# Query/key products directly behind their step's score pair, and their low parts ahead of the two maxima

## The reference

```python
h = _rmsnorm(x, norm_scale)
q = jnp.einsum('bsd,dhe->bshe', h, wq)       # 16 heads of 64
k = jnp.einsum('bsd,dhe->bshe', h, wk)
v = jnp.einsum('bsd,dhe->bshe', h, wv)
weights = jnp.einsum('bqhd,bkhd->bhqk', q * head_dim ** -0.5, k)
weights = jax.nn.softmax(weights, axis=-1)
new_vals = jnp.einsum('bhqk,bkhd->bqhd', weights, v)
out = jnp.einsum('bqhe,hed->bqd', new_vals, w_out) + b_out
...
x = _layernorm(x + _L0_attn_ref(x, ...))     # the first attention, above
x = _layernorm(x + _L0_ffn_ref(x, ...))      # 8 experts of 256, two chosen, and a shared one
x = _layernorm(x + _L1_attn_ref(x, ...))     # attention over the 16 heads of one token
x = _layernorm(x + _L1_ffn_ref(x, ...))      # 8 experts of 512, two chosen
```

## Time and profile before

| what | value |
|---|---|
| median of 3 runs | 1448.29 us (1448.22 to 1450.28) |
| the profiled execution, on the device | 1447.02 us |
| its span in the trace | 1445.2 us |
| TensorE matmuls busy | 1375.4 us, 95% of the span |
| TensorE weight loads busy | 1203.8 us, 83% |
| VectorE / ScalarE / GpSimd busy | 928.1 / 903.1 / 498.9 us |
| granted TensorE clock, mean | 0.988 |

### The profile page before, as it was taken

How to read it: one execution, slowest core, us unless ns; L and a number is a source line. 1 busy time by engine, 2 the same in 40 slices (tenths; PEclk the granted TensorE clock), 3 DMA queues, 4 the chain that set the end, 5 groups by cost and what they waited for, 6 DMA issues and landing times.

```text
span 1445.2 us, 33202 instructions
## 1 busy us (share of the span) xinstructions
PE 1375.4 (95%) x11328; PEld 1203.8 (83%) x11328; DVE 928.1 (64%) x2535; ACT 903.1 (62%) x2492; POOL 498.9 (35%) x409
## 2 busy tenths in 40 slices
PE   5797999999999999999999999999999999999768
PEld 4585989888898988889898898988889898888767
DVE  4456567575666757576675756667575675756683
ACT  4665775757566575766757576575757757575423
POOL 2307053160714417062350706225070531607100
PEclk9999999999999999999999999999999999999988
DMA  7000000000000000000000000000000000000000
GB/s 259 1 5 1 5 2 8 0 2 5 0 7 0 7 0 0 7 0 7 0 7 0 0 7 0 7 0 7 0 0 7 0 7 0 2 3 1 5 1 8
DMA packets 14088, 13.77 MB, mean 10 GB/s; under 512 B 1625, under 2 KB 12770, under 8 KB 13794
## 3 DMA queue, kind: packets, MB, share of 16 engines
q1 hardware_dynamic: 14050, 13.27, 2.9%
HBM read 11.17 MB, written 2.10 MB: 9 GB/s over the span
## 4 chain that ended last, share of the span: by engine, by line
PE 64%; issue 13%; DVE 8%; ACT 4%; DVEq 4%; POOL 3%; POOLq 2%; DMA 0%; SPq 0%; ACTq 0%
PE bank_F L1204 14%; PE bank_S L1074 6%; DVEq L343 4%; PE bank_T L1115 4%; PE bank_A L1128 4%; PE bank_T L1060 3%; ACT probs L566 3%; PE bank_A L1139 3%; PE bank_T L1061 3%; PE bank_T L1062 3%; PE bank_A L1060 3%; PE bank_A L1061 3%; PE bank_A L1062 3%; PE bank_F L1060 2%; PE bank_F L1062 2%
## 5 line engine op out<-in xcount | busy, mean ns | idle before, releaser
L1204 PE MATMUL bank_F<-down,hid 128*128 128x128 f32 x2944 | 356.0, 276 | 7.1 <-DVE x L783 6.4
L1204 PEld LDWEIGHTS bank_F<-down,hid 128*128 128x128 f32 x2944 | 341.5, 192 | 17.2 <-DVE x L783 9.9
L566 ACT ACTIVATE probs<-bank_S,neg_max 128x256 f32<-128x256 f32 x512 | 235.9, 475 | 143.6 <-DVE neg_max L704 143.6
L704 DVE TENSOR_REDUCE neg_max<-bank_S 128x2 f32<-128x512 f32 x256 | 164.7, 685 | 96.3 <-PE bank_S L1074 96.2
L783 DVE SCALAR_TENSOR_TENSOR x<-bank_F,gates,x 128x128 f32<-128x128 f32 x496 | 150.1, 344 | 42.5 <-PE bank_F L1204 32.7
L485 POOL TENSOR_TENSOR hid<-hid,qkv 128x1024 f32<-128x1024 f32 x60 | 169.1, 2828 | 22.7 <-ACT hid L582 22.7
L455 POOL TENSOR_TENSOR mean_sq<-sum_sq,one_over_d 128x2 f32<-128x2 f32 x16 | 3.1, 195 | 453.4 <-ACT h_row L540 453.4
L545 ACT ACTIVATE probsT<-bank_T 128x512 f32<-128x512 f32 x256 | 139.4, 605 | 28.0 <-PE bank_T L1115 28.0
L473 POOL TENSOR_TENSOR hid<-qkv 128x1024 f32<-128x1024 f32 x45 | 121.1, 2692 | 69.2 <-ACT qkv L545 69.2
L1139 PE MATMUL bank_A<-probsT,values 128*64 128x256 f32 x1024 | 140.4, 395 | 1.1 <-ACT probsT L545 1.0
L1115 PE MATMUL bank_T<-ident,probs 128*128 128x128 f32 x1024 | 138.3, 278 | 0.1
(11 more groups left out here) (191 smaller groups left out, 3233.2 us busy)
## 6 DMA issues: line engine op xcount, KB each, us to landing
x_row<-in_x SPq DMA_DIRECT2D x16, 128.0 KB, 2.1
down<-in_w SPq DMA_DIRECT2D x1, 2048.0 KB, 15.4
out<-x SPq DMA_DIRECT2D x16, 128.0 KB, 1.8
hid<-in_w SPq DMA_DIRECT2D x1, 1536.0 KB, 7.9
hid<-in_rw SPq DMA_DIRECT2D x1, 1024.0 KB, 7.4
hid<-in_wv SPq DMA_DIRECT2D x1, 512.0 KB, 3.9
hid<-in_wq SPq DMA_DIRECT2D x1, 512.0 KB, 4.8
hid<-in_wk SPq DMA_DIRECT2D x1, 512.0 KB, 5.5
```

What stands on the lines that cost most here:

```text
L566: ins = sc.activation(probs[:, h // 2 % 2, h % 2, t, :], unit.bank(f"S{h}")[:, t * S:(t + 1) * S], ACT.Exp, bias=neg_max[:, h, t:t + 1], a ...
L704: ve.tensor_reduce(neg_max[:, h, :], v.bank(f"S{h}")[:, :].rearrange("p (t k) -> p t k", t=NT), AX.X, ALU.max, negate=True).then_inc(max_r ...
L1204: ins = te.matmul(bank[:, (j * NT + t) * P:(j * NT + t + 1) * P], hid[:, e, k, tokens(t)], down[:, e, k, :], start=k == 0, stop=k == m - 1)
```

## The change

Two moves. In TensorE's list the unit `QK{s+3}` stands directly behind the score pair of step `s`, ahead of `O{s-1}` and the transposes, and no longer behind the transposes. In VectorE's step `lower_qk(s + 2)` stands ahead of the two maxima and no longer behind them. No instruction is added or taken away on any engine. ScalarE's list keeps its order.

```diff
@@ -87,11 +87,11 @@
         put("A", "QK2", on=a and s == 0)
         put("S0", f"S{2 * s + 2}", on=a and s + 1 < HP)
         put("S1", f"S{2 * s + 3}", on=a and s + 1 < HP)
+        put("A", f"QK{s + 3}", on=a and s + 3 < HP)
         put("A", f"O{s - 1}", on=a and s >= 1)
         put("F", *fill_units(it, s, 0))
         put("T0", f"T{2 * s}", on=a)
         put("T1", f"T{2 * s + 1}", on=a)
-        put("A", f"QK{s + 3}", on=a and s + 3 < HP)
         put("A", "HT", on=nxt and s == HP - 2)
         put("F", *fill_units(it, s, 1))
     put("A", f"O{HP - 1}", "OUT", on=a)
@@ -925,12 +925,11 @@
                 for s in range(HP):
                     if v.b and s == 3:
                         ln_apply(v, 1, x2, 1)
+                    if v.a and s + 2 < HP:
+                        lower_qk(v, s + 2)
                     if v.a and s + 1 < HP:
                         head_max(v, 2 * s + 2)
                         head_max(v, 2 * s + 3)
-
-                    if v.a and s + 2 < HP:
-                        lower_qk(v, s + 2)
                     if v.b and s == 0:
                         mix(v, "D0p1", 0, (2, 3), x2, x1, not v.a)
```

## The result

The changed kernel takes 1587.54 us (1584.82 to 1588.44), the kernel before, run beside it, 1448.78 us. The ratio is 1.0953 with a 95% interval of 1.0934 to 1.0972: 139 us slower. The prediction said slower, by 69 us, and 1538 us at most. The direction and nearly all waits were as predicted; the predicted loss was half of what came.

The account below looks back on a forecast made before the run. TensorE's own list was taken as the bound. Terms of 4.45 us a row over 15 rows, 66.8 us, plus 2.6 for row 0 made 69.4; added to 1447.0, plus 1.3 to the median, 1517.7 us, range 1498 to 1538.

Parts of the forecast that it names:

- row 0: First row, without fill units: `spread` of its step 5 gets the new wait, 2.6 us lost, bounds 0 and 4.45.
- 15 x 1.7: Waits in steps 3 and 4 over 15 rows: QK6 0.85, `spread` 0.2, QK7 0.8, less QK7's present wait 0.15 us.
- step 3 to 4: QK6 waits 0.85 us for the low part in step 3; `spread` of step 4 waits 0.2 us.
- step 4 to 5: QK7 waits 0.8 us, less its present wait of 0.15; `spread` of step 5 waits 0.95 us.
- `spread` of step 1: TensorE waits there for QK3's drain, ending with VectorE's low part of pair 3: stall of 2.2 us a row.
- the 0.2 us at `spread` of step 4: TensorE waits there for the scaling of O2, late because ScalarE's copy of x2's transpose is late: 0.2 us.
- Step 5, `spread`: TensorE waits for the low part of pair 7, queued behind VectorE's product of 1.27 us: 0.95 us a row.
- "No loss nor gain" behind step 5: Steps 6 and 7 have no QK unit; their VectorE chain moves with step 5's scores: neither loss nor gain.
- The credit of 0.4 us: Step 1: the mix comes 0.6 us earlier against the scores, so D0p3's wait goes: -0.4 us a row.
- The rival on the clock: The clock falls too: a 3 us half-clock stretch loses 1.5 us in each of 15 rows; 1540 us, chance 0.08.

Follow-up runs that it names:

- GpSimd late in after: Kernel after, with two small additions on GpSimd ahead of its second product so that VectorE's product starts first: 1552.41 us.
- banks kept: Kernel after, with every unit in the bank it had before and two small additions on GpSimd ahead of its second product: 1496.21 us.
- VectorE's half: Kernel before, with only the low part moved ahead of the maxima, plus two small additions on GpSimd ahead of its second product: 1469.71 us.
- GpSimd late in before: Kernel before, with only two small additions on GpSimd ahead of its second product: 1458.40 us.
- the tool: Two small additions on GpSimd ahead of its second product, result unused; alone on the kernel before: 1458.40 us.
- both undone: Kernel after, with two small additions on GpSimd ahead of its second product and unused matmuls (14 ahead of step 1, 6 ahead of step 5): 1533.90 us.
- VectorE's half alone: Kernel before, with only the low part moved ahead of the two maxima on VectorE, GpSimd unchanged: 1498.84 us.
- the version from the result: Kernel before, with VectorE's mixes of the older rows moved ahead of the maxima in steps 1, 2 and 5: 1441.88 us.
- TensorE's half alone: Kernel before, with only the QK units moved on TensorE, every unit in its old bank, VectorE's order untouched: 1630.21 us.

## Why the prediction was half right

The ladder of runs splits the 139 us, each rung being one edit (medians):

| from, to | us | what it is | predicted, 15 rows and row 0 |
|---|---|---|---|
| after to GpSimd late in after, 1587.5 to 1552.4 | 35 | product held off by GpSimd, and the clock lost with it | 0 |
| to banks kept, 1496.2 | 56 | re-dealt banks: `spread` of steps 1 and 5 | 15 x 3.15 + 2.6 = 50 |
| to VectorE's half, 1469.7 | 26.5 | TensorE's new order: QK units | 15 x 1.7 = 25.5 |
| to GpSimd late in before, 1458.4 | 11 | VectorE's new order | 15 x -0.4 = -6 |
| to before, 1448.8 | 10 | the tool | - |

The table says what each edit is worth in this order of undoing; the differences aren't strictly additive, since a stall can hide another edit's cost. Two of the rungs are known to be off. The tool's 10 us are those of the kernel before, where step 6 to 7 grows from 5.23 to 5.93 us; in the kernel after it stays at 5.17 us with the tool, so the first rung is 35 us, and some 3 more for the 0.2 us that the tool adds at the end of a row in either kernel. And VectorE's half carries that price while "banks kept" does not (6.00 and 5.29 us for the same step), so TensorE's new order costs, by estimate, 0.7 us a row more than its rung says, some 35 us.

A second account needs no ladder. It sets the steps of a row side by side, as means over rows 4 to 12 of the starts of `spread` in each trace (with both undone, over the seven of these rows that were undisturbed):

| stretch of a row | before | after | GpSimd late | both undone | predicted change |
|---|---|---|---|---|---|
| step 1 to 2 | 6.36 | 6.59 | 7.61 | 6.07 | -0.4 |
| step 2 to 3 | 7.77 | 7.96 | 7.96 | 7.96 | 0 |
| step 3 to 4 | 5.39 | 6.44 | 6.44 | 6.45 | 1.05 |
| step 4 to 5 | 5.85 | 9.76 | 7.65 | 7.65 | 1.6 |
| step 5 to 6 | 4.95 | 6.95 | 5.01 | 5.00 | 0 |
| step 6 to the last `spread` | 11.13 | 11.04 | 11.05 | 11.06 | 0 |
| from there to step 1 of the next row | 43.95 | 45.66 | 46.35 | 46.35 | 2.2 |
| row | 85.40 | 94.41 | 92.07 | 90.54 | 4.45 |

**The waits were right, and part of the closeness in the ladder is luck.** In row 6 it is 2.20 us for 2.2 at `spread` of step 1 and 1.06 for 1.05 from step 3 to 4. Each wait that came has the releaser that the prediction named; the 0.2 us at `spread` of step 4 did not come. TensorE was the bound, and of the stalls only 0.6 us a row were taken up later. The banks' rung is 56 us for 50, but not of the same things: it holds 1.5 us a row of lower clock behind step 1 (7.61 against 6.07 us), which the prediction left out, and it lacks 0.8 us for QK4, which waits only once the stall ahead of it is gone. Row 0 lost 3.7 us where 2.6 were predicted (the scores of step 0 of row 1 start at 93.20 and not at 89.51); the "0.47 us it waits now" in that working are the scaling and its hand-over, the wait itself is 0.53 us.

**Step 5, `spread`, was mis-sized.** The step said that the product "starts at 546.06 and takes 1.27 us". The start was right: set against `spread` of step 3 the product starts at 546.07 (599.59, less the 53.52 us by which that `spread` starts later). The duration was copied from the earlier trace rows. It belongs to the order of VectorE and GpSimd in the kernel before, which had 0.14 us of margin. The prediction moved ScalarE's copies by 1.41 us, from which GpSimd starts, and the exponentials, behind which VectorE's product starts, by 1.64 us. Both came (1.44 us for GpSimd's product, 1.65 for VectorE's). The difference of 0.23 us is more than the margin, so its own numbers turn the order round; but it wrote only that GpSimd's products are late "by less than TensorE is", without asking which of the two would now be first. What came is a wait of 2.94 us, not 0.95. With the order restored it is 0.81 us, so the rest of that step's working was good.

**"No loss nor gain" behind step 5 failed by the clock alone.** TensorE ran at the lower level behind the long wait, 1.58 us from step 5 to 6 in row 6 and 2.0 us in the mean. With product and clock undone, the steps behind step 5 are within 0.1 us of the kernel before, so VectorE's order costs nothing there in the changed kernel. Its rung of 11 us is a price in the kernel before, 0.5 us a row, and not one wait carries it: at `spread` of step 7 it is 0.66 us with VectorE's half and 0.59 us in the control. That the low part of pair 7 makes VectorE's chain longer there by its 0.68 us fits in size but is argued only.

**The credit of 0.4 us has two sides.** After the stall of step 1 D0p3's wait did go (-0.29 us from step 1 to 2). Without that stall, in VectorE's half alone, it stayed at 0.27 us. So what was taken as a gain of VectorE's order is mostly the stall having given the mix time. What makes the mix early by itself is to move the mix, as in the version from the result.

**The rival on the clock had the wrong weight.** It was given 0.08 and 1540 us. Row 1 had been read as the precedent, and set aside because that stretch had more idle time in it. In the kernel after the clock fell behind step 5 of the steady rows, and behind step 1 in about one of three. Filling the idle stretches gives 27 us back in the kernel after, and 18.5 us once the product is short. The rival's estimate of 22 us was a good size. The Trainium skill, "TensorE: Matmul & The Clock Gate", section "A second HAM failure mode: psum-queue depth-cycling", which the prediction weighed, says that pauses between groups, as TensorE cycles PSUM banks, can make the clock swing. This trace agrees, with 28 stretches at 1.2 GHz against 5 before; but not all pauses do it: with three of 0.7 or 0.8 us in each row ("the banks kept, with GpSimd late") the steady part stayed at 1.00.

**The miss, row by row.** A row is 9.0 us longer and not 4.45. Of the 4.6 us between, the held-off product is 2.1 (9.76 against 7.65 us from step 4 to 5) and the clock 2.5 (0.5 behind step 1, 2.0 behind step 5, after against both undone). The small terms make 0.5: 0.1 of the credit, 0.2 each from step 2 to 3 and from step 4 to 5. Against them stand the 0.6 us that come back at the row's end.

## What to carry to other kernels

When a unit moves within a list that deals out buffers in turn, write down for every wait behind it who had the buffer before and when that one is drained; here the re-dealing cost 3.7 us a row, and the move itself some 2.3. Where one engine is busy 99% of a stretch, hardly a stall is taken up later, so give an instruction's idle slot to work whose input is already there: ahead of the maxima the mixes won 6 us, where the low part, whose input ScalarE delivers at the end of its step, lost 11 even with the product kept short. That the input is what decides is argued from this pair of runs, not shown by itself. A duration read from a trace holds only while its neighbours on VectorE and GpSimd keep their order; when a change slides one against the other by more than the gap between their starts, cost the instruction at the other's full length.

## What the runs showed of the hardware

- In the steady rows VectorE's product of 128x1024 elements takes 1.22 to 1.29 us when it starts 0.13 us or more ahead of GpSimd's, and 3.13 to 3.38 us when it starts 0.06 to 0.31 us behind. In most rows of TensorE's half alone it starts 1.01 us behind and takes 2.43 us. Half a microsecond put in front of it cost 25 us in the whole kernel. The reported time of the instruction includes the time that it is held off, so it shows as busy and not as idle.
- Two additions on GpSimd of a few elements each cost the kernel before 10 us, by way of another pair of instructions (0.51 to 1.19 us on VectorE). In the changed kernel that pair doesn't meet (0.42 us).
- The clock fell in steady, otherwise dense rows. Time at the lower level: 131 us with waits of 2.0 and 2.9 us in a row, 182 us with four of 1.98 us, 101 us with 2.0 and 0.8 us, 87 us with one of 2.2 us; but 51 us with waits of 2.0, 0.5 and 1.6 us, 46 us with three of 0.7 or 0.8 us, and 33 us with one of 1.1 us, near the 35.5 us before. The kernels with re-dealt banks have two waits of 0.7 us besides. The runs don't say what separates the 51 from the 87 or the 101.
